# Attention's output product from high and low parts, one core of Trainium2

## What is computed

```python
q = (x @ Wq).reshape(b, n, 8, 64)
k = (context @ Wk).reshape(b, m, 8, 64)
v = (context @ Wv).reshape(b, m, 8, 64)
attn = softmax(einsum('bihd,bjhd->bhij', q, k) * SCALE)
out = einsum('bhij,bjhd->bihd', attn, v).reshape(b, n, 512)
return out @ Wout + bout          # Wout is 512 x 256
```

## Time and profile before

| what | value |
|---|---|
| median of 3 runs | 2096.34 us |
| the profiled execution's own time | 2094.84 us |
| its span, first to last instruction | 2093.1 us |
| PE busy | 1973.9 us (94%) |
| VectorE busy | 1533.5 us (73%) |
| GpSimd busy | 1488.2 us (71%) |
| ScalarE busy | 1255.7 us (60%) |
| mean granted TensorE clock | 0.974 |

### The profile page before, as it was taken

How to read it: one execution, slowest core, us unless ns; L and a number is a source line. 1 busy time by engine, 2 the same in 40 slices (tenths; PEclk the granted TensorE clock), 3 DMA queues, 4 the chain that set the end, 5 groups by cost and what they waited for, 6 DMA issues and landing times. The chain is left out here.

```text
span 2093.1 us, 51690 instructions
## 1 busy us (share of the span) xinstructions
PE 1973.9 (94%) x14320; PEld 1772.8 (85%) x14320; DVE 1533.5 (73%) x3647; ACT 1255.7 (60%) x3478; POOL 1488.2 (71%) x1695
## 2 busy tenths in 40 slices
PE   8999799999999999786999999999999999389997
PEld 6888578888887888676999999999999999368886
DVE  7888567877877877764777788888888888335554
ACT  5555465665665665434777777777777777224443
POOL 5555424777777777663888888888888888459764
PEclk9999899999999999898999999999999999789999
DMA  4300123233233233205777776777767777266542
GB/s 145 91 0 0 35 90 133 82 111 131 81 118 124 81 111 111 91 22 183 232 242 239 241 239 221 237 234 235 236 225 237 230 239 238 94 251 237 189 168 101
DMA packets 244909, 329.95 MB, mean 158 GB/s; under 512 B 50074, under 2 KB 167234, under 8 KB 244836
## 3 DMA queue, kind: packets, MB, share of 16 engines
q1 hardware_dynamic: 218788, 279.97, 41.1%
q0 software_dynamic: 26048, 49.10, 6.5%
HBM read 236.17 MB, written 77.18 MB: 150 GB/s over the span
## 5 line engine op out<-in xcount | busy, mean ns | idle before, releaser
L1359 POOL DMA_INDIRECT slot_token<-a_entry,a_slot_i x256 | 262.1, 1024 | 112.6 <-issue 70.3
L1821 POOL DMA_INDIRECT part_rows<-e_out,e_dest x184 | 224.4, 1220 | 70.9 <-issue 59.0
L2380 POOL DMA_INDIRECT x<-x_rows,tok x188 | 206.8, 1100 | 75.9 <-issue 56.1
L1952 ACT ACTIVATE e_sg<-e_g 128x256 f32<-128x256 f32 x368 | 141.6, 385 | 179.4 <-PE e_g L1672 178.0
L2001 DVE TENSOR_TENSOR e_h<-e_sg,e_u 128x256 f32<-128x256 f32 x368 | 157.3, 427 | 108.1 <-PE e_u L1672 52.6
L1184 ACT ACTIVATE a_prob<-a_s,a_ntop 128x128 f32<-128x128 f32 x512 | 180.8, 397 | 3.0 <-DVE a_ntop L1544 2.8
L1829 POOL TENSOR_TENSOR e_wd1l<-x,e_wd1h 128x256 fp32r<-128x256 f32 x184 | 145.5, 828 | 5.7 <-ACT e_wd1h L1932 4.8
L1829 POOL TENSOR_TENSOR e_wd0l<-x,e_wd0h 128x256 fp32r<-128x256 f32 x184 | 145.5, 829 | 5.4 <-ACT e_wd0h L1932 4.4
L2016 DVE TENSOR_SCALAR e_out<-e_d,e_dest 128x256 f32<-128x256 f32 x184 | 80.6, 479 | 71.4 <-PE e_d L1672 71.4
L1046 PE MATMUL a_o<-a_wo,a_ot 128*128 128x256 f32 x512 | 123.6, 385 | 8.4 <-DVE a_ot L1611 8.4
L1672 PE MATMUL e_d<-e_wd1h,e_ht1h 128*128 128x256 f32 x368 | 107.0, 291 | 24.5 <-issue 24.5
(11 more groups left out here) (395 smaller groups left out, 7578.4 us busy)
## 6 DMA issues: line engine op xcount, KB each, us to landing
x<-in_eg SPq DMA_DIRECT2D x94, 512.0 KB
x<-in_eu SPq DMA_DIRECT2D x94, 512.0 KB
x<-in_ed SPq DMA_DIRECT2D x93, 512.0 KB, 5.1
part_rows<-a_zero SPq DMA_DIRECT2D x16, 2048.0 KB
x<-part_rows SPq DMA_DIRECT2D x16, 2048.0 KB, 9.6
x<-in_x SPq DMA_DIRECT2D x16, 512.0 KB, 3.9
x_rows<-x SPq DMA_DIRECT2D x16, 512.0 KB
out_rows<-x SPq DMA_DIRECT2D x16, 512.0 KB, 10.3
```

The costliest lines, as they stand in the source:

```text
L1359: pool.indirect_dma_start(k.slot_tok, bass.IndirectOffsetOnAxis(ap=slot_i[:, j, q:q + 1], axis=0), entry[:, j, q, :], None, bounds_check=S ...
L1821: pool.indirect_dma_start(k.part_d, bass.IndirectOffsetOnAxis(ap=dest[a][:, n, 1:2], axis=0), out[a][:, n, :], None).then_inc(put[a], 16)
L1952: act.activation(sg[m % 2][:], bank_g[m % 2][:, 0:SETW], ACT.Silu).then_inc(sg_rdy, 1)
L2380: pool.indirect_dma_start(k.xg[a][:, n, :], None, k.x2_d, bass.IndirectOffsetOnAxis(ap=k.tok[a][:, n, 0:1], axis=0)).then_inc(k.rows_in[a] ...
```

## The change

The output product becomes a `split_product` of twelve fp32r matmuls. ScalarE copies `bank_v` as high part `oth` (`out_high`), VectorE subtracts it from the bank as low part `otl` (`out_low`), in the place of its copy. Both wait for the product of the slot before, `out_low` also for `out_high`. The weight is loaded raw at the head of SP's queue in the attention stage into the unused half of the second value buffer `vv1`, and is split once: the high part by ScalarE behind the first `weights`, the low part by VectorE behind the first `shares`; PE waits for that before the first output product. To make room, `blank` moves into the other half of `vv1` (PE waits for the table's stores before it makes the values that overwrite it), `plan` moves into a row of x that is free once all rows are stored, so its delivery now stands behind that wait, and three semaphores are merged into others.

```diff
@@ mixer_stage, sync @@
-                sp.dma_start(k.wo[:], dram["wout"].rearrange("(c p) n -> p c n", p=P)).then_inc(k.wp_in, 16)
@@ mixer_stage, scalar @@
-                        act.wait_ge(k.wp_in, 8 * 16)
+                        act.wait_ge(k.wp_in, 7 * 16)
@@ attention_stage @@
-        wo = k.wo
+        wo = [p.sb(f"wo{h}", [P, IC, D], F32R) for h in "hl"]
-        ot = p.sb("ot", [P, IC, T])
+        wo_raw = vv[1][:, 2:4, :].rearrange("p a (b d) -> p (a b) d", d=D)
+        oth, otl = (p.sb(f"ot{h}", [P, IC, T], F32R) for h in "hl")
+        wol_rdy, oh_rdy = p.sem("wol"), p.sem("oh")
+        WOH = ONE + 1
-        blank = p.sb("blank", [E + 1, SETW, 3], I32)
+        blank = vv[1][0:E + 1, 0:2, :].rearrange("p a n -> p (a n)")[:, 0:3 * SETW].bitcast(I32)\
+            .rearrange("p (n a) -> p n a", a=3)
@@ sync @@
+                sp.dma_start(wo_raw, dram["wout"].rearrange("(c p) n -> p c n", p=P)).then_inc(k.wp_in, 16)
+                sp.wait_ge(x2_out, DMA + 16 * NG)
                 plan.deliver(sp)
-                sp.wait_ge(x2_out, DMA + 16 * NG)
@@ tensor @@
+                            if m == 0 and isinstance(g, int) and g == 1:
+                                pe.wait_ge(blanked, DMA + 32)
-                    for m in range(IC):
-                        last = pe.matmul(bank_o[:, 0:D], ot[:, m, :], wo[:, m, :], start=(m == 0), stop=(m == IC - 1))
-                    last.then_inc(o_done, 1)
+                    split_product(pe, bank_o[:, 0:D], [((oth[:, m, :], otl[:, m, :]), (wo[0][:, m, :], wo[1][:, m, :]))
+                                                       for m in range(IC)]).then_inc(o_done, 1)
+                        if isinstance(s, int) and s == 1:
+                            pe.wait_ge(wol_rdy, 1)
                         out_rows(s - 1)
-                pe.wait_ge(k.wp_in, 8 * 16)
@@ scalar @@
+                def out_high(s):
+                    act.wait_ge(v_done, ONE + s + 1)
+                    if not isinstance(s, int) or s:
+                        act.wait_ge(o_done, ONE + s)
+                    act.activation(oth[:], bank_v[:].rearrange("p (m t) -> p m t", m=IC), ACT.Copy).then_inc(oh_rdy, 1)
                     emptied(g + 1, 1 - par, b, 1)
+                    out_high(s)
                     emptied(g + 1, 1 - par, b, 2)
                 weights(0, 0)
+                act.wait_ge(k.wp_in, 8 * 16)
+                act.activation(wo[0][:], wo_raw, ACT.Copy).then_inc(oh_rdy, 1)
@@ vector @@
+                def out_low(s):
+                    dve.wait_ge(oh_rdy, WOH + s + 1)
+                    if not isinstance(s, int) or s:
+                        dve.wait_ge(o_done, ONE + s)
+                    dve.tensor_tensor(otl[:], bank_v[:].rearrange("p (m t) -> p m t", m=IC), oth[:].bitcast(F32),
+                                      ALU.subtract).then_inc(ot_rdy, 1)
-                    dve.wait_ge(v_done, ONE + s + 1)
-                    dve.tensor_copy(ot[:], bank_v[:].rearrange("p (m t) -> p m t", m=IC)).then_inc(ot_rdy, 1)
+                    out_low(s)
                 shares(0, 0)
+                dve.wait_ge(oh_rdy, WOH)
+                dve.tensor_tensor(wo[1][:], wo_raw, wo[0][:].bitcast(F32), ALU.subtract).then_inc(wol_rdy, 1)
@@ first_tiles, build @@
+    k.plan = in_rows(k, SG + 7)[0:1, 0:4 * P * PARTS].bitcast(I32)
-        k.plan = sb("plan", [1, 4 * P * PARTS], I32)
-            k.wo, k.ctx_raw = kept("a_wo", [P, IC, D]), kept("ctx_raw", [P, 2, GW])
+            k.ctx_raw = kept("ctx_raw", [P, 2, GW])
```

More of the change, by code:

```diff
@@ L723, in deliver @@
         sp.wait_ge(self.plan_in, 16)
-        sp.dma_start(k.plan[:], k.plan_d.rearrange("w f -> (w f)").rearrange("(a n) -> a n", a=1))\
+        sp.dma_start(k.plan, k.plan_d.rearrange("w f -> (w f)").rearrange("(a n) -> a n", a=1))\
           .then_inc(self.plan_in, 16)
@@ L774, in attention_stage @@
         gates = p.sb("gates", [P, TG, K])
-        blank = p.sb("blank", [E + 1, SETW, 3], I32)
-        zero_rdy, filled, entry_rdy, spare_in = p.sem("zero_rdy"), p.sem("filled"), p.sem("entry"), p.sem("spare_in")
+        blank = vv[1][0:E + 1, 0:2, :].rearrange("p a n -> p (a n)")[:, 0:3 * SETW].bitcast(I32)\
+            .rearrange("p (n a) -> p n a", a=3)
+        filled, entry_rdy, spare_in = p.sem("filled"), p.sem("entry"), p.sem("spare_in")
         plan = Plan(k, p)
@@ L798, in attention_stage @@
         COUNTED = K + TG
-        blank_rdy, blanked, half_rdy = p.sem("blank_rdy"), p.sem("blanked"), p.sem("half_rdy")
+        blank_rdy, blanked = p.sem("blank_rdy"), p.sem("blanked")
         INVERTED, GROUPED, CHOSEN, STEPS = 2, 11, 15, 23
@@ L894, in _ @@
                 spare = zero[0:RT, None, :].to_broadcast([RT, TI, D])
-                sp.wait_ge(blank_rdy, 3)
+                sp.wait_ge(blank_rdy, 4)
                 each = blank[0:E].rearrange("p n a -> p (n a)")[:, None, :].to_broadcast([E, NSET, 3 * SETW])
@@ L899, in _ @@
                              blank[E:E + 1].rearrange("p n a -> p (n a)")).then_inc(blanked, 16)
-                sp.wait_ge(zero_rdy, 1)
                 sp.dma_start(k.x2_d[B * T:B * T + SETW, :].rearrange("(p n) d -> p n d", n=TI), spare).then_inc(spare_in, 16)
@@ L1147, in _ @@
             def _(act):
-                begin(act, e_rdy, t_out, ex_rdy, a_out[1], x2_rdy, ch_rdy, xh_rdy)
+                begin(act, e_rdy, t_out, ex_rdy, a_out[1], x2_rdy, ch_rdy, xh_rdy, oh_rdy)
                 act.sem_inc(ch_rdy, 2)
@@ L1268, in _ @@
             def _(pool):
-                pool.memset(zero[:], 0.0).then_inc(zero_rdy, 1)
+                pool.memset(zero[:], 0.0).then_inc(blank_rdy, 1)
                 begin(pool, xb_rdy, cl_rdy, ve_rdy, rs_rdy, nms_rdy, nrm_rdy, tok_rdy, mask_rdy, slot_rdy)
@@ L1272, in _ @@
                 pool.memset(blank[:], 0).then_inc(blank_rdy, 1)
-                pool.wait_ge(blank_rdy, 1)
+                pool.wait_ge(blank_rdy, 2)
                 pool.iota(blank[:, :, 0], pattern=[[1, SETW]], base=B * T, channel_multiplier=0).then_inc(blank_rdy, 1)
@@ L1278, in _ @@
                     .then_inc(entry_rdy, 1)
-                pool.memset(r_half[:], 0.5).then_inc(half_rdy, 1)
+                pool.memset(r_half[:], 0.5).then_inc(entry_rdy, 1)
                 plan.numbers(pool)
-                pool.wait_ge(half_rdy, 1)
+                pool.wait_ge(entry_rdy, 3)
                 def biased(g):
@@ L1348, in scatter @@
                             pool.wait_ge(slot_rdy, ONE + 2 * (r + 1))
-                            pool.wait_ge(entry_rdy, 2)
+                            pool.wait_ge(entry_rdy, 3)
                             pool.wait_ge(blanked, DMA + 32)
```

## The result

| | before | after |
|---|---|---|
| median | 2093.91 us (8 runs, 2091.97 to 2097.50) | 2101.41 us (8 runs, 2096.91 to 2107.25) |
| profiled execution, own time | 2094.84 us | 2107.25 us |
| mean granted TensorE clock | 0.974 | 0.973 |

The ratio is 1.0037, its 95% interval 1.0024 to 1.0050: the change costs 7.5 us, 0.37%. By the prediction's own bound of 0.3% that is slower, by a little; it had forecast +2.35 us, no change. Its time of 2098.7 us is 2.7 us too low and its range holds the result. But its sum started from a median of 2096.34 us, 2.4 us above the median before in this comparison, so the difference is 5.1 us too small, and the sum behind it does not describe what happened. The profiled execution after is the slowest of its eight, 5.8 us above their median; what follows is read from it.

What follows compares the result with a forecast made beforehand. Attention was taken as bound by PE, VectorE nearly as full. +0.30 us in 13 group crossings (+3.9), -0.8 for the first groups and -0.75 for the last product gave +2.35 us: 2098.7 us, range 2090.5 to 2106 us.

Steps and rivals of the forecast that it cites:

- the prediction's own bound of 0.3%: About 6.3 us, the smallest difference a measurement of this kernel was said to tell from no change.
- What bounds the kernel: Attention: PE sets 38.97 us per group, with VectorE nearly as full in one stretch, where the margin is 0.06 us.
- A to Q: Stretch from the end of weigh in slot b = 2 to the next queries' start: forecast 0.57 us longer, about 14.8 us.
- The hand-over: Slot b = 2: VectorE waits for ScalarE's copy, starts 0.63 us later, and the queries come 0.57 us later.
- The rival of VectorE's lateness costing twice: The delay meets PE at the queries and before q3: +0.8 us per group, 2105 us, chance 0.26.
- The step from plain to fp32r costs 0.18 us: PE's type change only moves ahead of the product in b = 0, 1, 3; new in b = 2, charged 0.11 us.
- Q to A: Stretch from the queries' start to the next group's weigh end in b = 2: forecast 0.27 us shorter, about 24.5 us.
- my own rival of shorter matmuls: Each of the twelve matmuls takes 0.022 us less: group -0.2 us, about 2092 us, chance 0.03.
- The first two groups and the last product: PE saves 0.13 us in each of six early slots, -0.8 us, and -0.75 us at the product standing alone.
- Split of the weight: Once, 1.04 us on ScalarE and 1.22 us on VectorE, covered by idle time: costs nothing, without cover 1 us.
- the signs that I named for a wrong forecast: A to Q of 14.2 us or less, a wait before q3, or a product not 1.4 us long.

Runs made afterwards that it cites:

- e5: The changed kernel without out_low's wait for the previous slot's product, and with the weight's low split moved from VectorE to GpSimd: 2090.91 us, 0.9981.
- e10: The changed kernel without out_low's extra wait or ScalarE's copy, VectorE's copy serving as both value parts, weight's low split on GpSimd: 2064.70 us, 0.9845.
- e2: The kernel before, plus one always satisfied wait per slot on VectorE ahead of its copy to ot: 2101.99 us, 1.0037.
- e1: The changed kernel without out_low's wait for the product of the slot before: 2114.60 us, 1.0090.
- e4: The changed kernel without out_low's extra wait and without ScalarE's copy, VectorE's copy serving as both value parts: 2085.35 us, 0.9957.
- e8: A second look at e4, unchanged: 2083.74 us in one run.
- e6: The kernel before, plus one idle VectorE instruction just ahead of the loop over groups: 2113.88 us, 1.0100.
- e11: The kernel before, plus 11 idle VectorE instructions at the head of the attention stage: 2104.49 us, 1.0050.
- e3: The changed kernel without out_low's extra wait, VectorE copying the whole bank after ScalarE's copy, plain fp32 product: 2116.89 us, 1.0102.

## Why the prediction was right or wrong

**What bounds the kernel** held. PE paces attention, and VectorE's queue from A to Q has no slack: the wait at Q came, 13 times, as the steps said.

**The hand-over** held. Forecast 0.63 us later on VectorE, 0.57 us on A to Q; e5 shows 0.49 us there, and e5 against e10 gives 0.66 us. In b = 0 I counted no wait before q3, with a bound of 0.15 us; of 13 groups of after, two have a short wait for `hit` there (0.39 and 0.41 us), both behind a turn of the loop, and e5 has none: it just fits. The rival of VectorE's lateness costing twice did not happen: slower came true, but by another mechanism than its own.

**"The step from plain to fp32r costs 0.18 us ... so this cost only moves"** failed. It is the mis-sized term. Where the product stands between transposes and fill in b = 0 to b = 1, TensorE's timeline of before is

```profile
464.74 1.03 PE L1039 MATMUL a_t<-ident,a_prob 128*128 128x128 f32 x8
465.61 1.89 PE L1046 MATMUL a_o<-a_wo,a_ot 128*128 128x256 f32 x8
467.15 2.64 PE L991 MATMUL a_a<-a_ct,wu_both 128*128 128x512 f32 x10
469.72 0.55 PE L1059 MATMUL a_v<-a_prob_t,a_vv 128*64 128x128 f32 x6
```

and that of after is

```profile
468.89 1.03 PE L1044 MATMUL a_t<-ident,a_prob 128*128 128x128 f32 x8
469.68 0.36 PE L1694 MATMUL a_o<-a_woh,a_oth 128*128 128x256 f32 x1
...
471.08 0.28 PE L1694 MATMUL a_o<-a_woh,a_otl 128*128 128x256 f32 x1
471.20 2.45 PE L994 MATMUL a_a<-a_ct,wu_both 128*128 128x512 f32 x10
473.58 0.66 PE L1063 MATMUL a_v<-a_prob_t,a_vv 128*64 128x128 f32 x8
```

From the transposes' start to the fill's start 2.41 us have become 2.31: the 0.13 us that I counted, nearly. But the fill behind it takes 2.38 us to `weigh` where it took 2.57. The time that I saw behind the plain product (0.18 us there, 0.19 here) belongs to what follows that product, and does not move in front of the new one, where small transposes stand. So a slot saves 0.29 us, not 0.13, in b = 2 too, where I had even charged 0.11 us. That turns Q to A from -0.27 into -0.67 us and the group from +0.30 into -0.18 us. It is the size that my own rival of shorter matmuls gave the group (-0.2 us), but not its mechanism: the product is 471.20 - 469.68 = 1.52 us from first start to the fill, made of the 0.12 us steps of the earlier trace rows and a first step of 0.20, and not the 1.16 us that I worked out from the Trainium skill, page "FP8 and Floating Point Precision", section "TensorE Precision Notes". That page's four passes for a true fp32 product the trace does not contradict: with the 0.19 us behind it the plain product takes 1.73 us, 0.108 us for each of sixteen passes, an estimate from that count. What was wrong is the price that I derived for an fp32r matmul, 0.097 us where the trace shows 0.12.

**The first two groups and the last product** had the right sign. In e5 the two groups take 36.78 and 37.35 us in place of 37.38 and 38.52, -1.8 us (forecast -0.8, again 0.13 and not 0.30 in a slot). In after they take 35.85 and 37.35, but there the stage starts otherwise: in e2, whose product is the old one, the first takes 36.43 us. The last product stands alone after too:

```profile
895.73 0.58 PE L1694 MATMUL a_o<-a_woh,a_oth 128*128 128x256 f32 x1 [7.46 <-DVE a_otl L1558]
...
898.46 0.82 PE L1096 MATMUL a_s<-ident,x 128*128 128x128 f32 x4
```

2.73 us against 3.57: -0.84 us, forecast -0.75.

**"Split of the weight ... Nothing"** and the waits that I counted only for what they wait for: here the prediction failed. I priced each added instruction by its duration and by who waits for it, and never by its place in VectorE's list. The split, 1.22 us once and hidden, and the second wait in `out_low`, satisfied when it is reached, moved the loop's body from 773 to 785 and lengthened it from 287 to 295. Either alone brings the gaps, as e1 (the split) and e2 (the waits) show. By the periods of the groups the two together cost 13.8 us.

**The sum, corrected:** 13 x -0.18 = -2.3, -1.8 for the first groups, -0.84 for the last product, +13.8 for the turns: +8.9 us, where the medians say 7.5. The two profiled executions differ by 12.4 us, but 3.0 of these lie ahead of the attention stage, whose first matmul starts at 242.59 us after and 239.55 before; that is not the change, as e4 and e8, one kernel, differ there by 2.3 us too. The turns' term comes from one execution, the slowest of eight. By the ratios to before, 1.0037 and 0.9981, the kernel after takes some 11.7 us more than e5, which has no turns' term. e5, which lacks the turns' term and the superfluous wait, should be 4.9 us faster than before; its medians say 4.05 us (2090.91 against 2094.96 us).

Of the signs that I named for a wrong forecast, one came, a wait before q3, twice, and only as a consequence of the turns. A to Q was to be about 14.8 us, and in undisturbed groups it is (14.7), and the product is 1.5 us long. What did not fit were five waits at Q of 2.0 to 2.8 us where 0.5 to 0.8 stood; no named sign looked at the loop's turn.

That 2098.7 us came so near is luck. Two errors of opposite sign met: -0.48 us in 13 groups (6.2 us, with 1.1 us in the first and last), and +13.8 us in five turns. They half cancelled, and what was left turned "no change" into a little slower.

## What to carry to other kernels

Price an added instruction by its place too: where an engine's list runs through a loop, look at the packets of the instruction queue and at gaps marked "issue" in front of the loop's first instruction, before and after each edit, and if they appear, move a once-only instruction to another engine or away from the loop. Before crediting or blaming an edit for half a per cent, run the kernel of before with the same number of idle instructions added to that engine. What a product costs is the distance from the start of what precedes it to the end of what follows it, not its own rows alone.

## What the runs showed of the hardware that was not expected

- One idle instruction of VectorE, executed once ahead of its loop, took 19 us (1.0% [0.84, 1.17]) in e6. Each turn of the loop then came with five packets of 8 KB and left VectorE idle for 2.6 to 3.6 us.
- The Trainium skill, page "Runtime: NRT & Kernel Launch", section "Instruction fetch mechanics", says that an engine other than PE holds two blocks of 16 KiB, 256 instructions each, filled in sequence, and that a taken branch to a target outside them has to fetch it first. By that rule a body of 287 instructions spans two blocks from most places and three from 287 - 257 = 30 of 256 of them, an estimate from this page. Where a block begins is not known here; if one bad stretch begins at 774, then 774 and 784 failing and 773 and 837 fitting go with it. No run here shows the size of a block or how many are held, and the packets speak against the page's 16 KB: they are 8 KB each, an odd number of them, 40 KB, in a turn. Pieces of 8 KB, half as many instructions, would fit the same places; by the same estimate a body behind 774 + 128 = 902 would be fetched again with them and not with the larger blocks. It was not run.
- Open is why the gap is 1.2 to 2.2 us for bodies that begin behind 784 or 785 and 2.2 to 3.6 us behind 774. With 287 instructions the later place has the shorter gap (e11 against e6); 295 were run only behind 784 and 785, and nothing was run between 774 and 784.
- A wait can cost PE its clock, and its length alone does not decide. In after 2.77 us of idling at Q were followed by nine matmuls at a step of about 0.42 us, the lower level, and a mean of 0.93 over the next 26.10 us; 2.56 and 2.20 us did the same. But 2.00 and 2.07 us left it at 1.00, and so did 2.85 us in e3 and 2.83 us in e6, where 2.35 us brought 0.93. With the waits of 0.70 us in e5 it stays at 1.00.
- Behind the plain fp32 product of 256 columns the same fill takes 0.19 us longer than behind the dozen fp32r matmuls (2.57 against 2.38 us).
